# Product-key experts: tokens normalised by ScalarE, moments and expert values taken earlier in a tile

## What is computed

```python
def _L0_ffn_ref(x, w_q, bn_gamma, bn_beta, keys, down_embed, up_embed):   # x is _layernorm(x)
    q = jnp.einsum('bnd,de->bne', x, w_q)
    ...                                     # batch-normalised over all tokens
    q = q.reshape(b, n, 2, H, KD).transpose(2, 0, 1, 3, 4)
    sim = jnp.einsum('pbnhd,hkpd->pbnhk', q, keys)
    sx, ix = jax.lax.top_k(sim[0], TOPK)
    sy, iy = jax.lax.top_k(sim[1], TOPK)
    all_scores = (sx[..., :, None] + sy[..., None, :]).reshape(b, n, H, TOPK * TOPK)
    ...
    scores, pk = jax.lax.top_k(all_scores, TOPK)
    ...
    h = jnp.einsum('bnd,bnhkd->bnhk', x, wd)
    h = gelu_new(h)
    h = jax.nn.softmax(scores, axis=-1) * h
    out = jnp.einsum('bnhk,bnhkd->bnd', h, wu)
```

## Time and profile before

| | |
|---|---|
| median of 3 runs | 4069.61 us (4067.66 to 4072.36) |
| the profiled execution | 4067.78 us, span 4066.0 us, mean granted TensorE clock 0.921 |
| busy share of the span | PE 85%, DVE 65%, ACT 42%, POOL 30% |
| the stretch of the changed block's tiles | from 398 to 1182 us of the span |
| busy in the tile from 818 to 842 us | PE 19.66, DVE 20.55, ACT 15.26, POOL 16.82 us of 24 |

### The profile page before, as it was taken

How to read it: one execution, slowest core, us unless ns; L and a number is a source line. 1 busy time by engine, 2 the same in 40 slices (tenths; PEclk the granted TensorE clock), 3 DMA queues, 4 the chain that set the end, 5 groups by cost and what they waited for, 6 DMA issues and landing times. The chain is left out here.

```text
span 4066.0 us, 81543 instructions
## 1 busy us (share of the span) xinstructions
PE 3440.8 (85%) x26798; PEld 2918.8 (72%) x26800; DVE 2662.2 (65%) x7388; ACT 1706.5 (42%) x4422; POOL 1223.8 (30%) x1672
## 2 busy tenths in 40 slices
PE   3886888888877888887889999999999999975666
PEld 2775777777765666645779999999999999834244
DVE  7674888888866888856435555555555455559776
ACT  1231666666645777755313333323333233313342
POOL 3553776666642333312200000000000000036042
PEclk8896999999988999988789999999999999968677
DMA  3000000000002222200121111111111111146000
GB/s 89 4 0 34 1 0 0 0 0 0 0 14 68 75 76 77 68 11 6 33 57 47 44 47 48 48 42 47 47 48 45 45 43 47 38 87 89 0 3 24
DMA packets 263508, 147.67 MB, mean 36 GB/s; under 512 B 111476, under 2 KB 259912, under 8 KB 262760
## 3 DMA queue, kind: packets, MB, share of 16 engines
q1 hardware_dynamic: 259048, 142.13, 13.2%
q10 hardware_dynamic: 4352, 4.20, 0.5%
HBM read 131.82 MB, written 13.65 MB: 36 GB/s over the span
## 5 line engine op out<-in xcount | busy, mean ns | idle before, releaser
L920 PE MATMUL psum<-L_ffn_share,L_ffn_prob 128*128 128x128 f32 x4096 | 508.4, 283 | 141.9 <-DVE L_ffn_prob L849 141.9
L920 PEld LDWEIGHTS psum<-L_ffn_share,L_ffn_prob 128*128 128x128 f32 x4096 | 488.2, 197 | 174.3 <-DVE L_ffn_prob L849 142.2
L2134 ACT ACTIVATE L_xattn_prob<-psum,L_xattn_nmax 128x258 f32<-128x258 f32 x512 | 239.3, 473 | 674.3 <-DVE L_xattn_nmax L2169 674.3
L744 POOL TENSOR_TENSOR L_ffn_sums<-L_ffn_sims 128x1024 f32<-128x1024 f32 x256 | 485.7, 1912 | 106.0 <-DVE L_ffn_prob L849 105.7
L2246 PE MATMUL psum<-L_xattn_ctxT,L_xattn_q_ctx 128*128 128x257 f32 x2048 | 487.7, 380 | 0.0
L2284 PE MATMUL psum<-L_xattn_probT,L_xattn_ctx 128*128 128x256 f32 x2048 | 484.6, 379 | 1.7 <-DVE L_xattn_probT L2187 1.7
L2187 DVE COPY L_xattn_probT<-psum 128x512 f32<-128x512 f32 x256 | 177.1, 692 | 391.4 <-PE psum L2270 391.4
L849 DVE SCALAR_TENSOR_TENSOR L_ffn_prob<-L_ffn_sums,L_ffn_best,psum 128x512 f32<-128x512 f32 x512 | 358.8, 742 | 104.8 <-ACT psum L777 99.3
L2109 POOL TENSOR_TENSOR L_xattn_z_var<-L_xattn_z_mv,L_xattn_z_eps 128x1 f32<-128x1 f32 x32 | 6.1, 192 | 1397.3 <-DVE L_xattn_z_mv L2201 1364.5
L2246 PEld LDWEIGHTS psum<-L_xattn_ctxT,L_xattn_q_ctx 128*128 128x128 f32 x2048 | 370.1, 191 | 48.1
L2284 PEld LDWEIGHTS psum<-L_xattn_probT,L_xattn_ctx 128*128 128x128 f32 x2048 | 370.1, 190 | 42.2 <-ACT L_xattn_lastT L2145 2.2
(11 more groups left out here) (440 smaller groups left out, 6545.4 us busy)
## 6 DMA issues: line engine op xcount, KB each, us to landing
L_xattn_ctxT<-ctx_T_dram SPq DMA_DIRECT2D x128, 257.0 KB, 2.8
L_xattn_ctx<-ctx_dram SPq DMA_DIRECT2D x128, 256.0 KB, 3.0
L_xattn_k_all<-ctx_T_dram SPq DMA_DIRECT2D x128, 128.5 KB, 2.1
L_xattn_v_all<-ctx_dram SPq DMA_DIRECT2D x128, 128.0 KB, 2.2
L_attn_qkv_scratch<-L_attn_qkv SPq DMA_DIRECT2D x24, 256.0 KB, 2.8
L_attn_rows<-L_attn_qkv_scratch SPq DMA_DIRECT2D x24, 256.0 KB, 5.2
start_raw<-ctx_dram ACTq DMA_DIRECT2D x16, 256.0 KB, 12.1
start_plug_all<-plug_scratch SPq DMA_DIRECT2D x1, 2048.0 KB, 7.2
```

What stands on the lines that cost most here:

```text
L744: nc.gpsimd.tensor_tensor(sums[:, h % RING, :, :], sx, sy, ALU.add).then_inc(summed, 1)
L920: last = nc.tensor.matmul(pair(2 * s)[:, c * P:(c + 1) * P], prob[:, h % RING, c * P:(c + 1) * P], share[:, h % RING, :], start=(h == 0 an ...
L2134: ins = nc.scalar.activation(prob[:, s, g, :], scores(s)[:, g, :], ACT.Exp, bias=nmax[:, s, g:g + 1], accum_out=total[:, s, g:g + 1])
```

## The change

The tokens of tile t + 2 are normalised by ScalarE as x * rstd + (-mean * rstd), after head 7, in place of VectorE. GpSimd computes the shifted mean -mean * rstd behind the power, and does all three operations between the sums of head 6 and of head 7 of tile t, in place of after head 1 of tile t + 1. VectorE takes the moments of t + 2 after the keep of head 2 in place of head 6. PE computes the expert values right behind `sim`, after head 1, with a wait for `mixed` (the weigh of the tile before, which reads the same PSUM banks), in place of after head 2 and behind `output`; and `output` stands after head 3, in place of head 2. ScalarE copies the transposed tokens after head 2 in place of head 1. PE's transposition stays after head 0. In the prologue both first tiles are normalised by ScalarE.

```diff
--- before.py
+++ after.py
@@ -707,10 +707,11 @@
         HALVES, HALF = 2, E // 2
         raw_prob = lambda k: core.psum[:, 4 + k, :]
         half = lambda t, k: t[:, k * HALF:(k + 1) * HALF]
+        shifted_mean = sb("shifted_mean", [P, S])
         front = Front(core, outer, f"{name}2", S, lambda s: core.psum[:, 7, 0:P])
-        (simmed, sims_ready, topped, paired, valued, squared, cubed, tanhed, gelued, cut, exped, inverted, shared, biased, summed, probs, used, kept,
+        (centred, simmed, sims_ready, topped, paired, valued, squared, cubed, tanhed, gelued, cut, exped, inverted, shared, biased, summed, probs, used, kept,
          mixed, out_done) = (core.sem(f"{name}_{n}") for n in (
-             "simmed", "sims_ready", "topped", "paired", "valued", "squared", "cubed", "tanhed", "gelued", "cut", "exped", "inverted", "shared", "biased", "summed", "probs", "used",
+             "centred", "simmed", "sims_ready", "topped", "paired", "valued", "squared", "cubed", "tanhed", "gelued", "cut", "exped", "inverted", "shared", "biased", "summed", "probs", "used",
              "kept", "mixed", "out_done"))
         block = outer.enter_context(nc.Block())
 
@@ -726,6 +727,12 @@
 
         @block.gpsimd
         def _(pool):
+            def normal_factors(t, s):
+                front.pool_rstd(pool, t - s, only=s)
+                pool.drain()
+                nc.gpsimd.tensor_scalar(shifted_mean[:, s:s + 1], front.mv[:, s, 0:1], front.rstd[:, s, :], -1.0, ALU.mult,
+                                        ALU.mult).then_inc(centred, 1)
+
             def pair_sums(t, s):
                 pool.wait_ge(topped, t + 1)
                 sx = top[:, s, 0:H, :].rearrange("p h (i j) -> p h i j", j=1).to_broadcast([P, H, TOP, TOP])
@@ -742,17 +749,23 @@
                     sx = sims[:, s, h, :].rearrange("p (i j) -> p i j", j=1).to_broadcast([P, K, K])
                     sy = sims[:, s, H + h, :].rearrange("p (i j) -> p i j", i=1).to_broadcast([P, K, K])
                     nc.gpsimd.tensor_tensor(sums[:, h % RING, :, :], sx, sy, ALU.add).then_inc(summed, 1)
-                    if after and h == 1:
-                        front.pool_rstd(pool, t + s, only=1 - s)
+                    if after == 2 and h == 6:
+                        normal_factors(t + 2, s)
                 if after:
                     pair_sums(t + 1, 1 - s)
 
-            front.pool_rstd(pool, 0, only=0)
+            normal_factors(0, 0)
+            normal_factors(1, 1)
             pair_sums(0, 0)
             over_tiles(pool, phase)
 
         @block.scalar
         def _(act):
+            def normalise(t, s):
+                act.wait_ge(centred, t + 1)
+                nc.scalar.activation(front.xn[:, s, :], core.x[:, ds(t, 1), :].rearrange("p a d -> p (a d)"), ACT.Identity,
+                                     bias=shifted_mean[:, s:s + 1], scale=front.rstd[:, s, :]).then_inc(front.normed, 1)
+
             def shift_exp(t):
                 act.wait_ge(cut, t + 1)
                 nc.scalar.activation(shift[:, :, :], shift[:, :, :], ACT.Exp).then_inc(exped, 1)
@@ -781,7 +794,7 @@
                     act.wait_ge(used, t * H + h + 1)
                     nc.scalar.activation(share[:, h % RING, :], core.c("ident"), ACT.Copy,
                                          scale=total[:, s, h:h + 1]).then_inc(shared, 1)
-                    if after and h == 1:
+                    if after and h == 2:
                         front.act_copy(act, t + s, only=1 - s)
                     if after and h == 4:
                         square(t + 1, 1 - s)
@@ -789,7 +802,11 @@
                         tanh(t + 1)
                     if after and h == 7:
                         shift_exp(t + 1)
-
+                    if after == 2 and h == 7:
+                        normalise(t + 2, s)
+
+            normalise(0, 0)
+            normalise(1, 1)
             front.act_copy(act, 0, only=0)
             square(0, 0)
             tanh(0)
@@ -851,6 +868,8 @@
                             best[:, s, h, TOP - 1:TOP], raw_prob(k), ALU.is_ge, ALU.mult).then_inc(kept, 1)
                     if before and h == 0:
                         weigh(t - 1, o)
+                    if after == 2 and h == 2:
+                        front.dve_moments(dve, t + 2 - s, only=s)
                     if after and h == 3:
                         add_bias(t + 1, o)
                         tops(o, range(0, KG // 2))
@@ -863,17 +882,12 @@
                         cube(t + 1, o)
                     if after and h == 6:
                         bests(t + 1, o)
-                    if after == 2 and h == 6:
-                        front.dve_moments(dve, t + 2 - s, only=s)
                 if after:
                     invert_totals(t + 1, o)
                     gelu(t + 1, o)
-                if after == 2:
-                    front.dve_normalise(dve, t + 2 - s, only=s)
 
             front.dve_moments(dve, 0, only=0)
             front.dve_moments(dve, 0, only=1)
-            front.dve_normalise(dve, 0, only=0)
             add_bias(0, 0)
             tops(0, range(KG)).then_inc(topped, 1)
             dve.wait_ge(paired, 1)
@@ -881,7 +895,6 @@
             bests(0, 0)
             invert_totals(0, 0)
             gelu(0, 0)
-            front.dve_normalise(dve, 0, only=1)
             over_tiles(dve, phase)
             weigh(TILES - 1, 1)
             dve.wait_ge(out_done, TILES)
@@ -925,10 +938,11 @@
                         front.pe_transpose(pe, t + s, only=o)
                     if after and h == 1:
                         sim(t + 1, o)
-                    if before and h == 2:
+                    if after and h == 1:
+                        pe.wait_ge(mixed, t)
+                        values(t + 1, o)
+                    if before and h == 3:
                         output(t - 1)
-                    if after and h == 2:
-                        values(t + 1, o)
 
             pe.wait_ge(experts_in, 32)
             pe.sem_inc(used, RING)
```

## The result

The changed kernel took **3968.1 us** (median of 4 runs, 3964.7 to 3974.5), the one before 4068.6 beside it: a ratio of **0.9755**, 95% interval 0.974 to 0.9771, so 100 us less. The profiled execution took 3974.47 us, span 3972.7, the slowest of the four.

The account below looks back on a forecast made before the run. It took a chain across engines, PE's order then VectorE's load, as the bound. Thirty tiles from 732.5 to 631.5 us, plus 1.2 at the end, gave 102 less: 4069.6 to 3967 us, range 3941 to 4006.

Parts of the forecast that it names:

- A cycle through PE's order and VectorE's load: Old loop tile, from one keep of head 1 (T) to the next: PE's order 10.74 us, then VectorE's load 13.35, together 24.09.
- The normalisation costs 1.88: VectorE's second half of a tile: moving the normalisation to ScalarE takes 1.88 us from the chain.
- The values and the square: Expert values earlier on PE: ScalarE's 3.58 us wait before its square goes, and with it VectorE's 2.68.
- The addition to x is late next, at T + 11.0: VectorE at head 5: the addition waits about 0.7 us for PE's output, until 11.0 us after head 1's keep starts (T).
- The second half, 10.05: From the addition to x to the next tile's keep of head 1: 10.05 us, as in old tile 30, including a 0.73 stall.
- A tile of 21.05: New loop tile, from one keep of head 1 to the next: 11.0 + 10.05 = 21.05 us, in place of 24.09.
- The falls of the clock go: PE's granted clock through the block: stays at 2.4 GHz as PE's gaps shrink, so 9.8 us of loss over 30 tiles goes.
- The first tile and the prologue, taken as 0: Start of the block: one short VectorE operation swapped for two on GpSimd and ScalarE, below 1 us either way.
- VectorE sets the pace: Rival, 8%: PE runs its order a little faster, so VectorE's addition to x never waits for the output; 3943 us.
- GpSimd late to L816: Rival, 11%: GpSimd's delay lengthens the stall of VectorE's subtraction L816 (L833 after the change) up to a whole sum; 4002 us.
- The square's wait stays: Rival, 2%: moving the values does nothing, as something else holds ScalarE; only 1.9 us a tile gained, 4012 us.
- slower by the clock: Rival, 5%: the clock falls to 1.2 GHz in PE's 10.1 us unbroken stretch; 4088 us if in 4 of 10 tiles.

Follow-up runs that it names:

- The two filler kernels: Eight matmuls of constants ahead of head 0, added to the kernel before with only PE's new order (4024.1 us) and to the kernel before itself (4058.7 us).

## Why the prediction was right

Forecast 3967, measured 3968.1: right in size, and in most of its steps; one cost was right in size and read as the wrong thing. Term by term:

- *A cycle through PE's order and VectorE's load*: shown. Values earlier takes 2.8 us out of the first half, normalisation on ScalarE 1.9 out of the second, each alone on the kernel before.
- *The normalisation costs 1.88*: the size is right, the reason is not. The prediction took it for VectorE's own load; L147 takes 0.35 us where nothing holds it, and about 1.5 us of the 1.88 were a stall on a GpSimd sum. So the prediction weighed such stalls only against the change (0.73 at L816). In fact the change took one such stall of about 1.5 us away and brought one of 0.75.
- *The values and the square*: 113.3 us of waiting to 7.5, as written.
- *The addition to x is late next, at T + 11.0*: measured T + 11.07. It waits 1.16, not 0.7, since VectorE's keep of head 5 began at T + 8.5 and not at 8.8. This moved no end.
- *The second half, 10.05*: measured 10.05 and 10.15 by turns. The stall is there: from the start of the best pairs (722.27) to L833's end went 2.15 us, as in tile 30 of before (2.14), with the 0.46 that stood idle ahead of L816 there now inside L833. So the test "L833 at 0.6" was badly put, its cost rightly. From L833's start to L835's it is 0.90, against 0.14 in the run with the values alone: 0.76, forecast 0.73.
- *A tile of 21.05*: measured 21.18 on average, (1047.23 - 433.06) / 29. That is 3.8 us over 29 tiles.
- *The falls of the clock go*: yes, 1.00 from 415.5 us to the block's end. The two filler kernels show the cause that the prediction argued. But "idle time shrinks, so the falls go" was a fair guess and no rule: with less idle time than before (0.59 and 2.52 for 1.52 and 2.62) they came in every tile, not in nine of thirty.
- *The first tile and the prologue, taken as 0*: **the mis-sized term**, 1.5 + 3.1 us. The first tile took 22.6, its L833 held for 1.99. Of the 3.1, 1.3 lie before the block's own work. Most of the rest is the first token tile: normalised by GpSimd and ScalarE, PE could transpose it only at 394.61 (392.62 before), and the copy then stood behind ScalarE's second normalisation (`sim` 2.6 later than before). Two more terms are not of the change's hops: the expert values took 3.62 us for 2.32, at a granted clock of 0.50 for 0.83, and the bias of the first tile took 1.89 us at 405.55, inside GpSimd's first sums. VectorE's shorter work (no normalisation, L833 at 0.59 for 1.46) gave part of it back. "One short operation for two" counted durations and not the hops between engines.
- *The last tile, 0*: from head 1 of tile 31 to the last addition 18.82 us in both.

Summed, the steps gave 102 us and the profiled executions differ by 93.3. The medians differ by 100.5, since the profiled run is the slowest of its four. So the agreement within 1.1 us is partly luck; within 9 us is what the steps earned.

Of the rivals, *VectorE sets the pace* (3943) is what happens if the output stays at head 2, only that the stall then grows: 3958. *GpSimd late to L816* (4002) is not the changed kernel's state, but the run with later small operations shows that price, a stall of nearly a whole sum, come by another way: 3992. *The square's wait stays* and *slower by the clock* were not seen, though the second's mechanism, one fall in every tile, is real: it took 0.86 us a tile in the run of PE's order alone (23.89 for 23.03), and after idle time, not in the long stretch of work.

What I missed: that most of the change does nothing in sum. The values' move alone gives 3971, within the spread of 3968. The later output and the collision at L833 ate the normalisation's 1.9 us a tile. And that most of this 1.9 was itself such a collision, which the rows of the kernel before show.

## What to carry to other kernels

Where a cycle runs through two engines, cost each part of a change alone as well as in sum: one part may give all of it and the others cancel. Before an instruction is moved for its price, compare its time in the loop with its time where nothing runs beside it (here 1.95 and 0.35): the difference is a wait that a busy share hides. When an instruction is on the chain and another engine's stream holds it, its price is set by where in that stream it falls (here 0, 0.75 or 1.6 us for the same instruction), so each edit that shifts either engine prices it anew, and two edits that fail alone may pay together. If TensorE waits for others in every tile, a few matmuls of constants in the gap are a cheap trial: they took 11 us here where the clock fell sometimes, and 28 where it fell in every tile.

## What was not expected of the hardware

- TensorE, idle 2.52 and 0.59 us once per tile, went down to the 1.2 GHz level in each of 28 tiles, 23.89 us apart; idle 2.62 and 1.52 us, in 9 places of the block. Why the one is regular and the other not stays open.
- A VectorE operation on eight elements a partition with one SBUF input took 0.16 us free, 0.92 in the middle of a GpSimd sum, and up to 1.94.
- A VectorE subtraction and multiplication of 128 x 128, with one SBUF input and two values a row, took 0.35 us free and 1.84 to 1.96 in most tiles of the loop, always ending 0.08 us behind a GpSimd sum.
- GpSimd holds on from one sum only to its end: with three sums back to back (5.65 us) L833 took 1.80, and never more than 1.99 in any tile of that run.
- ScalarE's normalisation, with a scale and a bias per row, took 0.49 us on 128 x 128, where the same with a scale alone is 0.39.
